# Attention and mixture-of-experts layer on eight cores: the router moved from the V projection into the attention stage, LayerNorm issued earlier, expert loads on another queue

## The reference

```python
xn = layernorm(x)
# attention, one head of width 1024, rotary on q and k, no mask
xq = rotary(xn @ wq.T); xk = rotary(xn @ wk.T); xv = xn @ wv.T
attn = softmax(xq @ xk.T / 32) @ xv
attn = attn @ wo.T
# experts: 2 shared (mid 512), 16 routed (mid 256), the best 2 weighted
out = sum(silu(xn @ wg_s[n]) * (xn @ wu_s[n]) @ wd_s[n] for n in range(2))
probs = softmax(xn @ router_w)                       # 16 columns
w, i = top_k(probs, 2); w = w / (w.sum() + 1e-9)
comb = one_hot(i) * w                                # tokens x 16
out += sum((silu(xn @ wg_r[e]) * (xn @ wu_r[e]) * comb[:, e]) @ wd_r[e] for e in range(16))
x = x + attn + out
```

## Time and profile before

| what | value |
|---|---|
| two timed runs | 4276.72 and 4532.12 us, median 4404.42 |
| the profiled execution | 4271.66 us, span of its slowest core 4270.1 us |
| spans of the eight cores | 4231.4 to 4270.1 us |
| PE busy | 3507.4 us (82%), 15904 matmuls |
| DVE busy | 1476.7 us (35%) |
| ACT busy | 595.9 us (14%) |
| chain that ended last | PE 70%, DMA 16%, DVE 6%, issue 4%, ACT 3% |

### The profile page before, as it was taken

The page is one execution under the profiler, slowest core; times in us unless marked ns, Lnnn a source line. Parts: engine busy times, 40 slices in busy tenths (PEclk is TensorE's granted clock), DMA queues, the critical chain, the costliest instruction groups (busy, mean ns, idle before and its releaser), DMA issues.

```text
span 4270.1 us, 49377 instructions; the slowest of 8 cores (4231.4 to 4270.1 us)
## 1 busy us (share of the span) xinstructions
PE 3507.4 (82%) x15904; PEld 1526.9 (36%) x15904; DVE 1476.7 (35%) x3713; ACT 595.9 (14%) x1475; POOL 22.5 (1%) x48
## 2 busy tenths in 40 slices
PE   3455555688888888888888869999999999999999
PEld 1121222233333333333333324444444444444443
DVE  3555443324343334333434222232323232323131
ACT  2222221011111111111111111010101010101010
POOL 0000000000000000000000000000000000000000
PEclk8776787889898889898989889999999999999999
DMA  4434799401010101010101064344344443434242
GB/s 110 137 128 134 141 136 125 101 6 55 6 55 6 55 6 55 6 55 7 54 9 41 10 177 146 140 144 143 144 143 148 138 158 128 168 119 178 95 171 89
DMA packets 109771, 412.59 MB, mean 97 GB/s; under 512 B 13088, under 2 KB 21280, under 8 KB 86832
## 3 DMA queue, kind: packets, MB, share of 16 engines
q1 hardware_dynamic: 105360, 361.15, 25.1%
q0 software_dynamic: 3008, 39.88, 7.1%
q10 hardware_dynamic: 1152, 8.39, 0.5%
HBM read 415.57 MB, written 58.85 MB: 111 GB/s over the span
## 4 chain that ended last, share of the span: by engine, by line
PE 70%; DMA 16%; DVE 6%; issue 4%; ACT 3%; SPq 0%; DVEq 0%; ACTq 0%; POOL 0%; POOLq 0%
PE pb L101 70%; DMA wdr_bf<-wdr 6%; DMA b_x<-x 3%; DMA f_wd<-wdr_bf 3%; DMA d_stl<-stab 2%; ACT d_P L101 2%; DVE b_st L101 1%; DVE d_OT L101 1%; DMA f_xnt<-xn_sp 1%; DVE d_O L101 1%; DVE d_qfm L101 1%; DMA c_rws<-rw 1%; DVE b_kswp L101 1%; DMA f_wgu<-wgu_bf 0%; SPq L101 0%
## 5 line engine op out<-in xcount | busy, mean ns | idle before, releaser
L101 PE MATMUL pb<-f_xnt,f_wgu 128*128 128x512 bf16 x4096 | 909.2, 380 | 33.7 <-DMA f_xnt<-xn_sp 27.7
L101 PE MATMUL pb<-Vs,d_PT 128*128 128x512 bf16 x2048 | 558.8, 411 | 92.4 <-DVE d_PT L101 92.4
L101 PEld LDWEIGHTS pb<-f_xnt,f_wgu 128*128 128x128 bf16 x4096 | 392.4, 98 | 520.3 <-issue 66.5
L101 PE MATMUL pb<-f_wd,f_h 128*128 128x512 bf16 x2048 | 462.6, 384 | 37.3 <-DMA f_wd<-wdr_bf 23.4
L101 PE MATMUL pb<-Kfm,d_qfm 128*128 128x512 bf16 x2048 | 458.8, 386 | 0.0
L101 DVE SCALAR_TENSOR_TENSOR f_uu<-pb,f_cb 128x512 bf16<-128x512 f32 x256 | 177.0, 692 | 571.4 <-PE pb L101 571.4
L101 DVE CAST d_PT<-pb 128x128 bf16<-128x128 f32 x1024 | 289.2, 290 | 241.4 <-PE pb L101 240.6
L101 ACT ACTIVATE f_sg<-pb 128x512 bf16<-128x512 f32 x256 | 153.0, 598 | 1324.6 <-PE pb L101 1233.3
L101 ACT ACTIVATE d_P<-pb,d_nmp 128x512 bf16<-128x512 f32 x256 | 172.9, 688 | 1044.5 <-PE pb L101 1044.5
L101 PEld LDWEIGHTS pb<-f_wd,f_h 128*128 128x128 bf16 x2048 | 195.2, 98 | 304.7 <-issue 92.5
L101 PEld LDWEIGHTS pb<-Kfm,d_qfm 128*128 128x128 bf16 x2048 | 203.3, 99 | 250.1 <-issue 16.5
(11 more groups left out here) (88 smaller groups left out, 2219.4 us busy)
## 6 DMA issues: line engine op xcount, KB each, us to landing
f_wgu<-wgu_bf SPq DMA_DIRECT2D x128, 1024.0 KB, 4.9
f_wd<-wdr_bf SPq DMA_DIRECT2D x128, 512.0 KB, 3.4
b_x<-x SPq DMA_DIRECT2D x32, 512.0 KB, 4.9
b_ct<-ctab SPq DMA_DIRECT2D x64, 256.0 KB, 3.4
b_stl<-stab SPq DMA_DIRECT2D x64, 256.0 KB, 3.9
wgu_bf<-wgu POOLq DMA_DIRECT2D x16, 1024.0 KB, 31.6
d_ct<-ctab SPq DMA_DIRECT2D x64, 256.0 KB, 3.3
d_stl<-stab SPq DMA_DIRECT2D x64, 256.0 KB, 3.6
```

What stands on the lines that cost most here:

```text
L101: inst = getattr(eng, meth)(*args, **kw)
```

## The change

Five edits:

1. In the K stage `emit_ln` for sub-tile `j/2` is recorded ahead of the table loads, the projection and the rope step of chunk `j`, and so ahead of `emit_xn` of the sub-tile before.
2. The router leaves the V stage. Its weights are loaded with the Q weights.
3. In the attention stage each tile begins with the four router groups (32 matmuls of 16 columns, banks 0 to 3) and four DVE copies of the logits into `d_lg4`; the DVE and ACT chain of a sub-tile is recorded behind its output projection. The transposed result (`emit_combT`: PE into bank 0, ACT out of it) comes one sub-tile later, for the last of a tile behind the next rope stretch, and is stored tile by tile (`spill_cbt`).
4. To make room, `d_qraw`, `d_qswp` and `d_O` become parts of one tile `d_sc2`, and all three names use its one `Buf`.
5. In the expert stage the loads of the first two experts' weights go to POOL's queue ahead of the shared weights; the combine weights come in 8 slices on SP.

```diff
@@ phase_b1
             for j in range(NCH):
+                if cur is not None and j % 2 == 0:
+                    emit_ln(cur, j // 2)
                 if prv is not None:
...
-                if cur is not None and j >= 2 and j % 2 == 0:
-                    emit_xn(cur, j // 2 - 1)
-                if cur is not None and j % 2 == 0:
-                    emit_ln(cur, j // 2)
                 if cur is not None and j >= 2:
-                    if j == 7:
+                    if j % 2 == 0:
+                        emit_xn(cur, j // 2 - 1)
+                    elif j == 7:
                         emit_xn(cur, 3)
@@ phase_b2
-        tok_wv = self.gload([(wvT[:, :], self.wT_d["wvT"]),
-                             (rws[:, :], self.rw_d)])
+        tok_wv = self.gload([(wvT[:, :], self.wT_d["wvT"])])
...
@@ phase_d
-        qraw = self.sb("d_qraw", [128, 512], BF16)
-        qswp = self.sb("d_qswp", [128, 512], BF16)
...
+        sc2 = self.sb("d_sc2", [128, D], BF16)
+        Ot = sc2
...
+        qraw = sc2[:, 0:512]
+        qswp = sc2[:, 512:1024]
+        tok_wq = self.gload([(wqT[:, :], self.wT_d["wqT"]),
+                             (rws[:, :], self.rw_d)])
...
+        def emit_combT(kc, pcm):
+            bcm = self.B("d_comb%d" % pcm)
+            tct = self.transpose(0, comb[pcm][:, :], waits=bcm.rd(),
+                                 out_parts=16)
+            bcm.read(self.mark("T", tct))
+            tcv = P.op("S", "copy",
+                       cbt[:16, (kc % 4) * 128:(kc % 4) * 128 + 128],
+                       self.pb[0][:16, 0:128],
+                       waits=self.pbf[0].rd() + [self._cbt_spill],
+                       inc="S")
...
+            for s4 in range(4):
+                q0 = s4 * 128
+                trt = self.mm_group(
+                    s4, self.pb[s4][:, 0:NE],
+                    [(xnt[:, c * 512 + q0:c * 512 + q0 + 128],
+                      rws[:, c * NE:(c + 1) * NE]) for c in range(NCH)],
+                    waits=bxt.rd() + [tok_wq])
...
                 pend = (j, bank, qraw, qswp, ct[pcs], st[pcs],
-                        "d_qraw", "d_qswp", "d_ct%d" % pcs,
+                        "d_sc2", "d_sc2", "d_ct%d" % pcs,
...
             qfm_w[pend[0]] = self.rope_step(*pend[1:], dst_w=wq0)
+            if self._cb_pend:
+                emit_combT(*self._cb_pend.pop(0))
+                spill_cbt(qt - 1)
...
+                if len(self._cb_pend) >= 1:
+                    emit_combT(*self._cb_pend.pop(0))
...
+        while self._cb_pend:
+            emit_combT(*self._cb_pend.pop(0))
+        spill_cbt(self.NTT - 1)
@@ phase_f
+        tok_gu = {}
+        tok_gu[0] = load_gu(0, g=True)
+        tok_gu[1] = load_gu(1, g=True)
         t_oh = self.yd(onehot[:16, :], self.onehot_d)
```

More of the change, by code:

```diff
@@ L550, in phase_b2 @@
                     self.B("Vs").wrote(self.mark("S", tev))
[L551 to L569, removed]
@@ L619, in phase_d @@
         PT = self.sb("d_PT", [128, 4 * 128], BF16)
-        Ot = self.sb("d_O", [128, D], BF16)
         OT = self.sb("d_OT", [128, NCH * 512], BF16)
+        rws = self.sb("d_rws", [128, NCH * NE], BF16)
+        lg4 = self.sb("d_lg4", [128, 4 * NE], F32)
+        pe = self.sb("d_pe", [128, NE], F32)
+        msk = self.sb("d_msk", [128, NE], F32)
+        eq1 = self.sb("d_eq1", [128, NE], F32)
+        comb = [self.sb("d_comb%d" % i, [128, NE], BF16) for i in range(2)]
+        r6 = [self.sb("d_r%d" % i, [128, 1], F32) for i in range(5)]
+        cbt = self.sb("d_cbt", [16, 512], BF16)
+        sc2 = self.sb("d_sc2", [128, D], BF16)
+        Ot = sc2
         att = [self.sb("d_at%d" % i, [128, 512], BF16) for i in range(2)]
@@ L633, in phase_d, with spill_cbt @@
         self.B("d_nmp").wrote(self.mark("V", t0m))
+        self._rt_v_last = None
+        self._rt_s_prev = [None] * 4
+        self._cb_pend = []
+        self.tok_cbsp = []
+        self._cbt_spill = None
+        self._cbt_copies = []
+        def emit_combT(kc, pcm):
[8 more added lines that the diff above has]
+                       inc="S")
+            self.bank_read(0, self.mark("S", tcv))
+            self._cbt_copies.append(self.mark("S", tcv))
+        def spill_cbt(tile):
+            tspc = self.yd(self.cbsp_d[:16, tile * 512:tile * 512 + 512],
+                           cbt[:16, :], waits=self._cbt_copies)
+            self._cbt_copies = []
+            self._cbt_spill = tspc
+            self.tok_cbsp.append(tspc)
         for qt in range(self.NTT):
@@ L642, in phase_d @@
                 tldx = self._dxn_next
+            for s4 in range(4):
[5 more added lines that the diff above has]
+                    waits=bxt.rd() + [tok_wq])
+                bxt.read(self.mark("T", trt))
+                tlg = P.op("V", "tensor_copy",
+                           lg4[:, s4 * NE:(s4 + 1) * NE],
+                           self.pb[s4][:, 0:NE],
+                           waits=self.pbf[s4].rd() + [self._rt_s_prev[s4]],
+                           inc="V")
+                self.bank_read(s4, self.mark("V", tlg))
             bqf = self.B("d_qfm")
@@ L858, in phase_f, with load_gu @@
         acc = [self.sb("f_acc%d" % i, [128, D], F32) for i in range(2)]
+        def load_gu(e, g=False):
+            bw = self.B("f_wgu%d" % (e % 2))
+            w = self.tok_conv + bw.begin()
+            if g:
+                t = self.gload([(wgu[e % 2][:, :], self.wgu_bf[e])], waits=w)
+            else:
+                t = self.yd(wgu[e % 2][:, :], self.wgu_bf[e], waits=w)
+            bw.wrote(t)
+            return t
+        tok_gu = {}
+        tok_gu[0] = load_gu(0, g=True)
+        tok_gu[1] = load_gu(1, g=True)
         t_oh = self.yd(onehot[:16, :], self.onehot_d)
         self.bufs["f_onehot"].wrote(t_oh)
-        t_cb = self.yd(combT[:16, :], self.cbsp_d, waits=[self.tok_cbsp])
-        self.bufs["f_combT"].wrote(t_cb)
+        t_cbt = [self.yd(combT[:16, tt * 512:tt * 512 + 512],
+                         self.cbsp_d[:16, tt * 512:tt * 512 + 512],
+                         waits=[self.tok_cbsp[tt]])
+                 for tt in range(self.NTT)]
         prs = []
@@ L893, in emit_cb @@
             bcb = self.B("f_cb%d" % (e % 2))
[L894 removed]
+            w0 = (bf.begin() + [t_cbt[tt]] +
                   self.B("f_onehot").rd())
```

109 lines of the change are left out of this document (37 added, 72 removed).

## The result

Changed kernel against the kernel before on the same chip: the ratio of the times is 1.0192, 95% interval 1.0146 to 1.0238. The profiled executions took 4349.72 us (span 4348.1, core 1) and 4271.66 us: +78, where the prediction had +92. The median over all 12 timed executions was 4434.81 us (before: 4384.64 over 10) and lies above my range of 4320 to 4415: in seven of the 12, and in five of the 10 before, the cores of a die ran at a lower clock, which the ratio leaves out, and the other five of the changed kernel took 4334.82 to 4371.23 us.

A forecast was written before the change was run, and what follows sets the result against it. PE's waits were taken to bound the kernel, with POOL's queue ending the V stage and DVE pacing the rope stretch. K -4, V 0, attention +108, expert -12 gave +92 on 4271.66: 4364, taken as 4366; range 4320 to 4415.

The forecast's parts named there:

- Over 2% slower: Whole kernel: outcome class holding most of the main forecast, Rival C and Rival D; chance 0.55.
- K stage: K stage: tile 0 +9 us, tiles 1 to 7 -13 us, together -4; bounds +6 and -33.
- V stage: V stage: POOL's conversions set its end, so moving the router gains 0 us; bound -2.
- pace of the rope step: Attention rope stretch: shared Buf delays ACT's copy 1.14 us, own-engine wait adds 0.18; 2.66 to 3.98 us a step.
- last `d_at` to first score: Attention tile boundary: router chain and slower rope steps put the first score at +35.1 us against 23.6, +11.5.
- bank 0 and clock, a tile: Attention stage: two more turns through bank 0 before scores, +1.4 us, and lower clock stretches, 0.5 us a tile.
- expert stage: Expert stage: PE starts some 19 us after the barrier instead of 34, part given back: -12 us, bounds 0 and -22.
- Rival A: Attention stage: chain beside PE's work, own-engine wait free, no clock loss; 4343 us, chance 0.27.
- Rival C: Attention stage: slower rope stretch drops PE's clock, 4 us a tile, 32 us; 4398 us, chance 0.15.
- Rival B: K stage: all of ACT's waits for x leave the path, giving 124 us back; 4244 us, chance 0.06.
- Rival D: Expert stage: the new loads leave PE's start where it is; 4378 us, chance 0.07.
- The rule on queues: Expert loads: SP and POOL transfers share 16 engines; if two queues gave nothing, the sum would be some 10 us more.

The follow-up runs named there:

- after: The changed kernel with all five edits, against the kernel before: ratio 1.0192.
- a_sep: The changed kernel with separate Bufs for the two halves of `d_sc2`, otherwise as changed; ratio 1.0021 against the kernel before.
- a_xfirst: The changed kernel with `f_xnt` of tile 0 issued on SP ahead of onehot and the combine-weight slices; lower of two executions 4338.79 us.
- b_fpool: The kernel before with the weights of experts 0 and 1 on POOL's queue ahead of the shared weights, combine weights one load; ratio 0.9973.
- b_drain: The kernel before with each attention rope step's second DVE operation also waiting for the first; lower of two executions 4262.14 us.
- b_conv: The kernel before with the 32 expert-weight conversions moved from the V stage to the attention stage, behind each tile's rope stretch; ratio 0.9895.
- b_best: The kernel before with new LayerNorm order from tile 1, two raw buffers, conversions in the attention stage, expert weights on POOL; 4133.66 and 4144.65 us.
- b_rconv: The changed kernel with old LayerNorm order, old expert loads and separate Bufs, plus conversions moved into the attention stage; ratio 0.9731 against the kernel before.

## Why the prediction came out as it did

The median of 4434.81 us lies outside my range, and the step that put it there is the last one of the sum. I noted that the median before (4404.42) was of two runs, 4276.72 and 4532.12, and then added the +92 to the lower one alone: 4366 is a forecast of the low end of the executions, and the range was laid around it. The runs showed the low end at 4334.82 and the profiled execution at 4349.72, both in the range, and the medians of the two kernels, 4384.64 and 4434.81, far above their low ends.

For the change itself the mechanism was right where the time went, the shared `Buf` and the chain at the tile boundary, and the sum was 14 us too large for the profiled execution. "Over 2% slower", to which I gave 0.55, is not shown: 1.0192, with an interval of 1.46 to 2.38% slower. The steps, with means over kernels of the same code where there are any:

| step | predicted | measured |
|---|---|---|
| K stage | -4 | -11.4 on the profiled cores; -3.3 over medians |
| of it tile 0 | +9 | +8.0 (first projection 44.33 to 52.32); +8.5 over medians |
| of it tiles 1 to 7 | -13 | -11.8 (-3.3 less 8.5) |
| V stage | 0 | -0.1 |
| pace of the rope step | 3.98 | 4.06 |
| last `d_at` to first score | +11.5 | +12.0 |
| bank 0 and clock, a tile | +1.9 | +0.2 |
| tile 0 of the attention stage | +8 | +8.8 (60.6 less 51.8) |
| end of the attention stage | +6 | +5.8 (8.8 from the last `d_at` to the barrier, before 3.0) |
| expert stage | -12 | -7 on the profiled cores; -9.5 over medians (1803.2 of after and a_sep, less 5.8 of the end, against 1806.9) |

- **The K stage** held as a sum and as a mechanism: the late load is gone and its place is taken by PE's wait for `b_kraw`. The 11.4 us of the profiled cores would have been read as an error of mine, but they are mostly the difference between two cores. My sum for a cycle gave 14.7 us and the one shown takes 14.08, before 14.28, so this cycle got no slower. And the bound of +6 for the stage does not follow from its terms: with no late load saved, tile 0 gives +9 and the slower cycles 0.4 x 3 x 7 = 8 more.
- **The term of the sum that was mis-sized** is the turn through bank 0 and the clock, 1.9 us a tile, 13 us in all. PE does idle 0.53 in each turn (15.9 us in 30 waits on ACT `d_cbt`). The first 64 scores of tiles 1 to 7 take 15.97 us in the mean where they took 15.44 (15.87 with one Buf alone, 15.09 with the router alone, so this goes with the slower rope stretch). Both effects are there; but from a tile's first score to its last `d_at` it takes 185.3 us, and before 185.1 (means of all tiles and cores). Something in the sub-tiles gives most of it back; I could not say what, and no run isolates it. Without this term the sum would be +79, next to the measured +78. That would be luck as well: on the profiled cores the K stage came out 7 us below my term and the expert stage 5 above it.
- **The pace** was 0.08 short, 4.06 for 3.98: I had the own-engine wait at 0.18, and the first two operations stand 0.86 apart instead of 0.61.
- **The other mis-sized term** is the expert stage. I had PE start 19 us behind the barrier, and it was 23.3, since I charged the nine small loads 2 us and they took 5.3. By the run with `f_xnt` first these small loads cost 12 us of the start; what they cost at the end, 2 to 7, is not clear of the error.
- **The V stage** stood, but for half a reason. I wrote that POOL's queue sets its end and not DVE or the router. True of this kernel; the router was the next limit behind it.
- **Rival A** (less than charged at the boundary) had a number, 4343, that is nearer to 4349.72 than my 4364, and that is luck: the boundary grew by 12.0 us, more than I charged, the chain was not hidden, and the own-engine wait cost 0.20 a step, not nothing. Of its three parts only the smallest, the clock, lies in what fell away. **Rival C** (the clock, 4 us a tile) is out: the first scores of a tile take 0.5 us more, and the stage's granted clock is 0.89 in both. **Rival B** is out: the waits for x left the path, as it said, but the K stage gave 3 to 11 us and not 124, since PE then waited for `b_kraw`. **Rival D** is out by the earlier start.
- **The rule on queues** (the Trainium skill, DMA: Bandwidth & Descriptors, section Issuing engines are not separate DMA queues) is not contradicted. What a_xfirst gained came from the order within one queue; b_fpool changed queue and order together, so no run here tells what a second queue is worth.

## What to carry to other kernels

When two buffers are packed into one tile, give each part its own bookkeeping: memory may be shared without sharing the waits, and here the one name cost 76 us and the packed memory, by the pace of 2.66 with two Bufs in it, nothing. Whatever writes the whole tile, here `d_O`, must then wait for both. When work is moved out from under a longer transfer, nothing is gained until the transfer is moved too; look for the second limit before deciding that a stage "is not bound by it". And compare stages over all cores: one core of one execution was off by as much as the effect looked for.

## What the runs showed of the hardware that I had not expected

- A wait of DVE on its own preceding operation cost 0.19 us between starts (0.79 instead of 0.60), and 0.20 a rope step (b_drain).
- Eight transfers of 16 KB took SP's queue 4.1 to 4.9 us to issue on the eight cores of the changed kernel. Standing ahead of the 1 MB load of `f_xnt`, they made PE's first expert matmul 12 us later (31.1 against 18.8). POOL's queue issued eight large loads meanwhile (2537.07 to 2541.31); that these are the cause is my reading.
- Conversions on POOL's queue in the attention stage, right behind the rope stretch, made that stage differ by up to 45 us between cores (b_conv, 1682.5 to 1727.6). Issued behind the products of the first two sub-tiles it was 16 us with the router left (b_best, 1659.6 to 1676.0) and 13 with it moved (b_rconv, 1701.8 to 1714.9); the kernel before, without conversions there, has 20 (1681.3 to 1701.6).
- The same code differed between the cores of one execution by up to 20 us in the K stage (484.6 to 505.0).
